# Causal and banded masks added to attention scores by one product over 128 contraction partitions per bank instead of two over 64 each

## What is computed

```python
# layer 2, causal: 16 heads of d = 16, S = 512
scores = einsum('hbqd,hbkd->hbqk', Q_, K_) / d ** 0.5
scores = where(tril[None, None] == 0.0, NEG, scores)
attn = softmax(scores, axis=-1)

# layer 3, banded: W = 64
mask = (j <= i) & (i - j < W)
s = einsum('bhqd,bhkd->bhqk', q, k) / sqrt(DH) + bias[None]
s = where(mask[None, None], s, -1e9)
a = softmax(s, axis=-1)
```

## Time and profile before

| | us |
|---|---|
| median of 3 runs | 1596.85 |
| lowest and highest run | 1592.26, 6304.54 |
| profiled execution, its own time | 1590.74 |
| its span | 1588.9 |
| TensorE products busy | 1426.6 (90% of the span) |
| TensorE weight loads busy | 713.9 (45%) |
| VectorE busy | 864.6 (54%) |
| ScalarE busy | 716.6 (45%) |
| GpSimd busy | 263.6 (17%) |

### The profile page before, as it was taken

One profiled execution on the slowest core, in us unless ns is written; L12 is line 12 of the kernel. 1 busy time (PEld: TensorE's weight loads), 2 busy tenths in 40 slices (PEclk: granted clock), 3 DMA queues, 4 the chain that ended last, 5 costly groups with the idle time before them and its releaser, 6 DMA issues.

```text
span 1588.9 us, 23992 instructions
## 1 busy us (share of the span) xinstructions
PE 1426.6 (90%) x8204; PEld 713.9 (45%) x8232; DVE 864.6 (54%) x2099; ACT 716.6 (45%) x1177; POOL 263.6 (17%) x138
## 2 busy tenths in 40 slices
PE   5999898888999988888999998988899998988886
PEld 2336555423533654543443464553263355455334
DVE  2663565585266256567355536556636635655762
ACT  0663353455366234427446425352825632625462
POOL 1004131301100413220110213121011041303001
PEclk9999999989999989998999998998999999999898
DMA  9000404303200230540310031242031005043210
GB/s 339 22 1 12 102 1 91 70 14 113 68 1 7 38 70 1 99 75 1 126 55 1 8 62 45 38 86 51 1 127 54 1 8 106 2 71 64 41 60 14
DMA packets 44776, 85.28 MB, mean 54 GB/s; under 512 B 10464, under 2 KB 27872, under 8 KB 44384
## 3 DMA queue, kind: packets, MB, share of 16 engines
q1 hardware_dynamic: 41136, 73.17, 18.6%
q10 hardware_dynamic: 3504, 10.39, 3.2%
HBM read 43.68 MB, written 2.10 MB: 29 GB/s over the span
## 4 chain that ended last, share of the span: by engine, by line
PE 62%; DVE 15%; issue 10%; ACT 5%; SPq 3%; DMA 3%; ACTq 1%; POOL 0%; DVEq 0%; POOLq 0%
PE ring L1286 8%; PE obank L1296 8%; PE ring L1276 7%; DVE nmax L1075 7%; PE ring L1463 6%; PE ring L1252 6%; PE ring L1352 4%; PE ring L1603 3%; PE obank L1513 3%; PE ring L1201 3%; ACT q_all L771 3%; PE ring L1454 2%; SPq L413 2%; DVE rbuf L1094 2%; DMA q_all<-q_parts 1%
## 5 line engine op out<-in xcount | busy, mean ns | idle before, releaser
L1075 DVE TENSOR_REDUCE nmax<-ring 128x2 f32<-128x1024 f32 (+1 forms) x192 | 218.5, 1175 | 51.3 <-PE ring L1463 33.7
L679 ACT ACTIVATE region_e<-region_d,nmin 128x512 f32<-128x512 f32 x256 | 182.6, 714 | 83.7 <-DVE nmin L936 82.6
L936 DVE CUSTOM_DVE_ANT_0 region_d<-ring,maskb 128x512 f32<-128x512 f32 x256 | 165.9, 686 | 91.5 <-issue 89.4
L784 ACT ACTIVATE region_e<-ring 128x1024 f32<-128x1024 f32 x192 | 183.4, 992 | 55.7 <-PE ring L1463 32.7
L771 ACT ACTIVATE q_all<-ring 2x1024 fp32r<-2x1024 bf16 x96 | 97.6, 1016 | 204.7 <-PE ring L1524 204.2
L606 POOL TENSOR_TENSOR nat_x<-nat_n,rows 128x1024 f32<-128x1024 f32 x16 | 37.6, 2353 | 606.1 <-DVE nat_n L985 461.2
L1286 PE MATMUL ring<-region_q 64*128 64x512 f32 x512 | 126.9, 615 | 6.7 <-ACT region_q L668 5.4
L1454 PE MATMUL ring<-cbf 64*128 64x128 bf16 (+2 forms) x1280 | 131.7, 286 | 0.0
L1071 DVE TENSOR_REDUCE nmax<-ring 128x4 f32<-128x512 f32 (+1 forms) x96 | 86.1, 911 | 75.0 <-PE ring L1454 74.3
L1296 PE MATMUL obank<-region_e,vs 128*64 128x512 f32 x512 | 124.0, 605 | 0.0
L780 ACT ACTIVATE region_e<-ring 128x768 f32<-128x768 f32 (+1 forms) x96 | 74.0, 776 | 55.1 <-PE ring L1454 52.8
(11 more groups left out here) (193 smaller groups left out, 2171.4 us busy)
## 6 DMA issues: line engine op xcount, KB each, us to landing
q_all<-q_parts SPq DMA_DIRECT2D x192, 64.0 KB, 2.5
region_e<-in_w_f SPq DMA_DIRECT2D x8, 1024.0 KB, 5.8
k_tiles_a<-k_parts SPq DMA_DIRECT2D x96, 64.0 KB, 2.3
k_tiles_b<-k_parts SPq DMA_DIRECT2D x96, 64.0 KB, 2.3
q_all<-q_parts ACTq DMA_DIRECT2D x96, 64.0 KB, 3.2
wvo<-in_wv SPq DMA_DIRECT2D x5, 1024.0 KB, 5.1
wqk<-in_wq SPq DMA_DIRECT2D x4, 1024.0 KB, 9.1
wqk<-in_wk SPq DMA_DIRECT2D x4, 1024.0 KB, 11.1
```

The costliest lines, as they stand in the source:

```text
L679: ins = act.activation(e0[:, n % E0, h, :], sm0[:, n % 2, h, :], ACT.Exp, bias=nmin0[:, n, h:h + 1], scale=-1.0, accum_out=sum0[:, n, h:h ...
L784: act.activation(e16[:, n % 4, 2 * u:2 * u + 2, 0:nq], slot((a, "B", g, kt, u))[:, :, 0:nq], ACT.Exp)\
L936: ins = dve.tensor_tensor_reduce(out=sm0[:, n % 2, h, :], in0=slot(("S0", p, kt))[:, h, :], in1=maskb[:, :], scale=-1.0, scalar=3.0e38, op ...
L1075: dve.tensor_reduce(nmax[:, qt, 2 * u:2 * u + 2], slot(name)[:, :, 0:nk], AX.X, ALU.max, negate=True)\
```

## The change

The mask is added by one product over all 128 partitions per bank. `mask_heads` has two products instead of four; its stationary operand is the whole identity. The tables have one copy of each mask and `halves` is gone, so the array of constants has 1416 columns instead of 2312, of which 1280 instead of 2176 are cast to bf16.

```diff
-CONSTS = [("ident", P), ("halves", 2 * P), ("maskA", 2 * P), ("maskB", 2 * P), ("bandA", 2 * BAND), ("bandB", 2 * BAND),
+CONSTS = [("ident", P), ("maskA", P), ("maskB", P), ("bandA", BAND), ("bandB", BAND),
           ("keyrows", S), ("slopes", 2 * GROUPS), ("tri", P)]
...
-                def mask_heads(dst, n, table, part, cols):
-
-                    for half in range(2):
-                        for i in range(2):
-                            own = slice(64 * i, 64 * i + 64)
-                            mask = cb(table, cols.stop - cols.start, own, at=half * part + cols.start).unsqueeze(1).broadcast_to(
-                                [64, n, cols.stop - cols.start])
-                            ins = pe.matmul(dst(i), cb("halves", P, own, at=half * P), mask, start=False, stop=(half == 1),
-                                            skip_group_check=(n == 2))
+                def mask_heads(dst, n, table, cols):
+
+                    mask = cb(table, cols.stop - cols.start, at=cols.start).unsqueeze(1).broadcast_to([P, n, cols.stop - cols.start])
+                    for i in range(2):
+                        ins = pe.matmul(dst(i), cb("ident", P), mask, start=False, stop=True, skip_group_check=(n == 2))
                     return ins
...
-    put_halves("halves", (p == x).astype(np.float32))
-    put_halves("maskA", np.where(x > p, NEG, 0.0))
-    put_halves("maskB", np.where(p > x, NEG, 0.0))
+    put("maskA", np.where(x > p, NEG, 0.0))
+    put("maskB", np.where(p > x, NEG, 0.0))
     ahead = y - W - p
-    put_halves("bandA", np.where((ahead <= 0) & (ahead > -W), 0.0, NEG))
+    put("bandA", np.where((ahead <= 0) & (ahead > -W), 0.0, NEG))
     behind = y - p
-    put_halves("bandB", np.where((behind >= 0) & (behind < W), 0.0, NEG))
+    put("bandB", np.where((behind >= 0) & (behind < W), 0.0, NEG))
```

More of the change, by code:

```diff
@@ L1479, in pass_a @@
                     if a == BANDED:
-                        ins = mask_heads(lambda i: by_head[:, i, :, :], len(us), "bandA", BAND, slice(BAND - nk, BAND))
+                        ins = mask_heads(lambda i: by_head[:, i, :, :], len(us), "bandA", slice(BAND - nk, BAND))
                     elif a == CAUSAL:
-                        ins = mask_heads(lambda i: by_head[:, i, :, nk - P:nk], len(us), "maskA", P, slice(0, P))
+                        ins = mask_heads(lambda i: by_head[:, i, :, nk - P:nk], len(us), "maskA", slice(0, P))
                     ins.then_inc(*ends_fill(name))
@@ L1496, in pass_b @@
                     if a == BANDED:
-                        ins = mask_heads(lambda i: by_head[:, i, :, :], len(us), "bandB", BAND, slice(0, nq))
+                        ins = mask_heads(lambda i: by_head[:, i, :, :], len(us), "bandB", slice(0, nq))
                     elif a == CAUSAL:
-                        ins = mask_heads(lambda i: by_head[:, i, :, 0:P], len(us), "maskB", P, slice(0, P))
+                        ins = mask_heads(lambda i: by_head[:, i, :, 0:P], len(us), "maskB", slice(0, P))
                     ins.then_inc(*ends_fill(name))
```

## The result

| | before | after |
|---|---|---|
| median in the comparison, 4 runs each, us | 1597.09 | 1655.07 |
| ratio, 95% interval | | 1.036 [1.0327, 1.0393] |
| profiled execution, its span, us | 1588.9 | 1655.8 |
| mean granted clock of TensorE in it | 0.965 | 0.934 |

The kernel became slower by 57 to 58 us, 3.6%. The forecast was 1616 us with a range up to 1632, so the time lies outside, on the side of the rivals A and B.

What follows compares the result with a forecast made beforehand. TensorE was taken as the bound, with 62% of the chain. Shape changes in causal stages (15.8 us) and banded ones (11.1), less 2.2 at the start, gave +24.7 on 1590.74: 1616 us, range 1603 to 1632.

Steps and rivals of the forecast that it cites:

- A: Masked stages: TensorE's clock falls once more in each of eight, 14 us more, 1630 us; chance 0.11.
- B: Masked stages: covers give out, 144 jobs off the path also pay the way in, 12 us more, 1628; chance 0.12.
- streamed columns and products: Mask products: halves already ran side by side, so merging them and halving the count saves 0 us.
- C: Masked stages: shape changes hide in waits for slots, only the start gains, 1588.5 us; chance 0.08.
- D: Mask products: pairs don't run side by side, so streams halve, some 66 us saved at most, 1525 us; chance 0.02.
- the price of the shape: Bank jobs: shape changes twice; extra 0.24 us causal, 0.285 banded, only 0.085 where values follow the mask.
- how much of it is on the path: Masked stages: 4.0 us per causal stage, 2.8 per banded one; 15.8 and 11.1 us over four of each.
- The constants: Kernel start: smaller table and shorter cast let TensorE start between 0.5 and 2.7 us earlier, taken as 2.2.
- The sum: Whole kernel: shape changes in causal and banded stages less the gain at the start, +24.7 us; chance 0.66.

Runs made afterwards that it cites:

- the second profiled execution: The changed kernel unaltered, measured once more in another comparison against the kernel before: 1641.86 us, ratio 1.0282.
- the first experiment: The kernel before plus one zero product of one column over 128 partitions behind the four mask products of every bank job: 1662.37 us, ratio 1.041.

## Why the prediction was wrong

**Right: streamed columns and products.** 640 products, 138.8 us against 131.7: neither the halved count nor the merged halves saved anything. C and D are out.

**Right: the price of the shape at 2.4 GHz.** TensorE's timeline of the changed kernel in the first causal and the first banded stage, which answer to the earlier trace rows.

```profile
210.08 0.50 PE L1459 MATMUL ring<-q_all,k_tiles_a 64*128 64x512 f32 x2
210.52 0.28 PE L1451 MATMUL ring<-cbf 128*128 128x128 bf16 x2
210.73 0.44 PE L1459 MATMUL ring<-k_tiles_b,q_all 64*128 64x384 f32 x2
211.11 0.29 PE L1451 MATMUL ring<-cbf 128*128 128x128 bf16 x2
```

```profile
274.86 0.47 PE L1459 MATMUL ring<-k_tiles_a,q_all 64*128 64x192 f32 x4
275.26 0.50 PE L1451 MATMUL ring<-cbf 128*128 128x384 bf16 x2
...
276.09 0.50 PE L1451 MATMUL ring<-cbf 128*128 128x384 bf16 x2
```

Scores of 512 columns to mask: 0.44 us, expected 0.42, before 0.34. Mask to mask in the causal stage: 0.59, expected 0.58, before 0.35. In the banded stage: 0.83, expected 0.83, before 0.54. The rows of the full stage with its keep-warm products had this price right to 0.01 us per job. The scores' loads start when the scores do (both at 210.73 and at 275.69), not under the mask. The Trainium skill, TensorEngine Tiling (Array Packing), Key Properties, says that a changed tiling mode drains the engine; the trace agrees that the change costs, with 0.08 to 0.10 us on the way in. The Trainium skill, TensorE: Matmul & The Clock Gate (Single matmul latency), gives a drain of about 175 ns for a single product; as the price of a change of shape it is not borne out. The sum by it would have been about 1638 us, nearer to the result, but for a cause that the rows do not show.

**Nearly right: how much of it is on the path.** At a held clock a causal stage costs about 3.5 us more (expected 4.0), a banded one 2.3 to 2.4 (expected 2.8). The first chain pieces of the changed kernel answer to the earlier trace rows:

```profile
1.71 13.98 DMA region_e<-in_consts
...
15.72 0.83 DVE cbf L843
...
17.29 12.81 PE ring L1201 x24
```

The constants land 1.1 us earlier, the cast takes 0.83 us instead of 1.29, and TensorE starts 1.5 us earlier (expected 2.2, between 0.5 and 2.7). The sum is 23.4 - 1.5 = 21.9 us against 24.7 expected. The table's split gives much the same by another way, 1564 - 1542 = 22 (28 with the factor of 0.48 for the kernel before). B would have raised the stages' price at a held clock above the forecast; they came out below it.

**Wrong: the clock.** This is the step that failed. The sum has no term for the clock, and rival A, which has one, was put down as one more fall of 1.8 us in each of eight stages, 14 us in all with a chance of 0.11. The argument against it was that the longest waits, those for L771, stay as long as they are and that the products between them stream as many columns. These waits and columns did stay (1.39 us against 1.48, the same columns), though in the causal stages the wait ahead of L771 is as long; the conclusion that the clock stays did not hold. There are no more falls than before, seven of eight masked stages (eight in the second profiled execution), and they lie around the same waits, but a stage that fell then spends 10 to 34 us at the lower level instead of 3.4 to 6.8. In the masked stages that is 117 - 41 = 76 us more at 1.2 GHz, and these stages took 57.9 us more, of which 23.4 are the price of the shape: 34 us are the clock's. The other stages and layers took 9 us more, and the time at 1.2 GHz rose there by some 29 us; that the one is due to the other was not tried by itself. In the second profiled execution it was 2 us, with some 13 more at 1.2 GHz, so this part is not steady. So of the 67 us between the two profiled spans, 22 are the term that was worked out, 34 the clock in the masked stages, and some 11 lie elsewhere. Between the medians, 58 us apart, about 22 are again the term that was worked out, and the other 36 are what the sum did not have. The sign that the prediction named for A, a granted clock of the causal stages under 0.9, came in two of the four windows of causal stages, 0.87 and 0.88; the other two have 0.90.

What would have helped was in the rows before the change. The masked stages there spent nothing, 3.4 or 6.8 us at the lower level, so the way back already varied between stages of the same code; one fall was priced as if its length were given.

**What is shown, and what stays open.** Shown: that a one-column product of the other shape in each job, without the larger mask products, brings both the price and the lost clock (the first experiment); that filling the wait for L771 keeps the clock up in most masked stages and returns 40 of the 58 us, or 26 of the 47 of the second comparison, where it gives the kernel before 14. Not shown apart from the change of shape is what one more product with its load costs, and not shown apart from a shorter wait is what products around the wait do. Not settled is by what the chip decides when to raise the clock again: it stayed at 1.2 GHz for 34 us in which the profile has TensorE busy throughout, with a change of shape twice per job. That the gaps inside the changes of shape are what matters was only argued; they cannot be seen in busy time. Also open is why the length differs between executions (in the banded stages 68 and 48 us for the same kernel).

## What to carry to other kernels

A product that merges two halves of the partitions saves no columns where the halves already ran side by side, and if its neighbours keep another shape it pays twice per job for the change. Look for every place where the granted clock falls and ask whether the changed sequence of products could make the fall last longer: a fall is not an event of fixed price. Where TensorE sets the pace, try to fill a long wait near which the clock falls: four products that nobody reads made the kernel before 0.8% faster (1582.94 us, 0.9916 [0.9883, 0.9948], the best version here); in the full stage, where VectorE carries more of the chain than TensorE, filling brought a higher clock and no time.

## What the runs showed of the chip that was not expected

Added work made a kernel faster: with 32 products of 512 columns in the wait the changed kernel took 26 to 40 us less.

320 products of one column, each busy 0.18 us and in another shape than its neighbours, cost 65 us.

A microsecond at 1.2 GHz loses 0.42 us in the banded jobs of the changed kernel and 0.48 in those of the kernel before, not half. In the changed one the way from scores to mask went from 0.40 us (274.86 to 275.26) to 0.68 (670.44 to 671.12), so it did not double. The Trainium skill, TensorE: Matmul & The Clock Gate (HAM oscillation — how this bites in real kernels), counts half of the throttled time as lost; the pitches give somewhat less.
